# Two local-attention stacks: 48 rows in one sequence, each row's feed-forward cut into pieces beside the heads of later rows, weights loaded by parts

## The chip, the core and the metric

The kernel runs on one core of one Trainium2 chip. The metric is the device time of one execution in microseconds (us), the median of several executions. Below, PE is the matmul engine (TensorE), DVE is VectorE, ACT is ScalarE, POOL is GpSimd, and SP is the queue that issues the DMAs.

## What is computed

The input is 8 rows of 256 tokens with 128 features, in float32. Four blocks follow each other. Blocks 1 and 2 (0-based) end in a stack of six local-attention layers, and these two stacks are what the change is about. Cut to what matters:

```python
DIM, DEPTH, HEADS, DIM_HEAD, WINDOW = 128, 6, 16, 64, 32
DIM_INNER = 341

def attn_layer(x, Wqkv, qs, ksc, Wo):      # x is 8 rows of 256 x 128
    q, k, v = split(x @ Wqkv)              # 128 -> 3 * 1024, 16 heads of 64
    q, k = l2norm(q) * qs, l2norm(k) * ksc
    q, k = rotate(q), rotate(k)            # cos and sin tables, with a scale
    out = local_attention(q, k, v)         # window of 32, looks one window back
    return out @ Wo                        # 1024 -> 128

def ffn_layer(x, g, bln, W1, b1, W2, b2):
    xn = layernorm(x) * g + bln
    a, gate = split(xn @ W1 + b1)          # 128 -> 2 * 341
    return a * gelu(gate) @ W2 + b2

for i in range(DEPTH):
    x = attn_layer(shift_tokens(x), ...) + x
    x = ffn_layer(shift_tokens(x), ...) + x
```

The eight rows of a layer don't depend on each other. Row b of layer d+1 needs only row b of layer d.

## The kernel before

The stacks are `windowed_transformers`. Its inner `run(number)` emits one stack; it runs twice. The activations stand in the SBUF tile `Y`, one slice for each of the 8 rows. Work is ordered by hand: each engine has its own program, and the engines meet through semaphores. A **turn** is one row in one layer; turns count through a stack.

**The attention of a row** has two parts that overlap with its neighbours'.

- *Preparation* is spread over the eight pairs of heads of the row before it. PE makes 12 chunks of 512 columns of q, k and v (`pe_chunks`, L1518, two in each of the slots 0 to 5), ACT squares and copies them (L1661, L1665), DVE sums the squares and multiplies by the sine table (`dve_rotate`, L1762, L1770), POOL multiplies by the cosine table, adds, and scales the keys (`pool_prepare`, L1615, L1622, L1628), and PE transposes q and k (`pe_turn_qk`, L1544). In the slots 3 and 6 DVE takes 1/sqrt of the head norms by Newton steps (`dve_prepare`, L1786, then L704 to L710); each step waits for the step before. A short memset (L1788) then raises `rs_ready`, for which POOL's key scaling (L1628) waits.
- *The window* goes through eight pairs of heads p = 0 to 7: PE computes scores (L1450), DVE adds the mask and takes the maximum (L1731), ACT takes the exponential (L1638), PE transposes the probabilities (L1462, L1463), ACT copies them (L1647), PE spreads the reciprocals (L1477) and weighs the values (L1490). In pair 6 PE multiplies the previous row's context by Wo (`pe_out`, L1559). In pair 7 DVE adds that to `Y` (`dve_add`, L1794).

So `pe_window`, `act_window` and `dve_window` are the rows of one turn on the three engines. PE, ACT and DVE take their instructions strictly in the written order:

```python
for b in range(1, B - 1):
    pe_window(pe, turn + b, b % 2)
pe_window(pe, turn + B - 1, 1, last=True)
...
for b in range(B):
    pe_ff_step(pe, turn + b, b, b % 2, b == 0, b == B - 1, ...)
```

**The feed-forward** of a layer comes as a phase of its own, after the eighth row's attention: eight `pe_ff_step`s. A step shifts the next row's upper half of the features by one token (L1843, L1846), runs the 6 products with W1 (L1870), and the 6 with W2 (L1857). ACT shifts into `xn` (L1893), turns and scales the normed row (L276) and takes GELU (L1901). DVE takes mean and variance (L235 to L241), normalises (L245), multiplies the two halves (L1925), and adds to `Y` (L1918). POOL copies half a row (L1887) and takes the root of the variance (L252). The next layer's first row is prepared in this phase (`PREPARE_IN_FF`), and its other rows can't start in it. Exponential and GELU need different function tables in ACT: a table load stands ahead of each phase (L2020, L2028), so two in a layer.

**The loop.** Layers 0 to 4 of a stack run in a device loop (`Fori`), the sixth is written out behind it, without preparation in its feed-forward phase. SP loads the weights of a layer as whole tensors: Wqkv (1536 KB) once the layer before has finished its last preparation, and W1, W2 after its last feed-forward step.

The functions in full, with the profile's line numbers:

Of the kernel before, what the change touches and what calls it, by code (L numbers as in the profile page):

```python
# [81 lines left out]
def allocate(nc, ctx):  # L82
# [24 lines left out]
    c.next_row = sb("next_row", [P, HALVES, D])  # L107
# [1242 lines left out]
N_CHUNKS = len(CHUNK_ORDER)  # L1350
PE_CHUNK_SLOTS = {j: (2 * j, 2 * j + 1) for j in range(6)}
# [8 lines left out]
RSQRT_STEPS = 2 * (1 + NEWTON_STEPS)  # L1360


PREPARE_IN_FF = {2: ((0,), (1,)), 3: ((2,), ()), 4: ((3,), (4,)), 6: ((5, 6), ()), 7: ((7,), ())}

ATTN_FROM, FF_FROM = 2, B
SPAN = (P, P + WINDOW)
AT = (0, P)
FIRST_KEY = (0, P - WINDOW)


def windowed_transformers(nc, sem, c, name, io):
# [28 lines left out]
    hT = (c.hT, c.big[:, at:at + 3 * S].rearrange("p (k s) -> p k s", k=3))  # L1409
# [4 lines left out]
    ss = c.ss[:, :, :].rearrange("p t h -> p (t h)")  # L1414
    rs = tuple(c.rs[:, j, :, :].rearrange("p t h -> p (t h)") for j in range(2))

    def norms(buffer, g):
        return buffer[:, 32 * g:32 * g + 32]
# [4 lines left out]
    def whole_blocks(turned):  # L1423

        return turned.rearrange("p (t k) -> p t k", k=P + WINDOW)[:, :, 0:P]
# [4 lines left out]
    def chunk_bank(i):  # L1430
        return c.bank[7 - i % 2]

    def qkT_bank(i):

        return c.bank[7 - i % 2 if i < 2 or i >= 4 else 6 + i % 2]
# [3 lines left out]
    def pe_scores(pe, turn, j, p, first=False):  # L1439
        if p % 2 == 0:  # L1440

            pe.wait_ge(s.qT_copied, turn * 4 + p // 2 + 1)
            pe.wait_ge(s.kT_copied, turn * 4 + p // 2 + 1)
        if not first:

            pe.wait_ge(s.negmax_ready, turn * PAIRS + p)
        for t in range(HALVES):
            for side in range(2):
                q, k = [x[j][DH * side:DH * side + DH, p, :] for x in (qT, kT)]
                last = pe.matmul(c.bank[side][:, AT[t]:AT[t] + SPAN[t]], q[:, t * P:(t + 1) * P],  # L1450
                                 k[:, FIRST_KEY[t]:FIRST_KEY[t] + SPAN[t]], start=True, stop=True,
                                 skip_group_check=True)
        last.then_inc(s.scores_ready, 1)

    def pe_turn_probs(pe, turn, p, first):
        pe.wait_ge(s.probs_ready, turn * PAIRS + p + 1)
        if not (first and p == 0):

            pe.wait_ge(s.probsT_ready, turn * PAIRS + p)
        for side in range(2):  # L1460
            probs, out = c.pairs[:, 2 * (p % 4) + side, :], c.bank[2 + side]
            pe.transpose(out[:, 0:P], probs[:, 0:P], c.ident[:, :])  # L1462
            last = pe.transpose(out[:, P:2 * P], probs[:, P + WINDOW:2 * P + WINDOW], c.ident[:, :])  # L1463
        last.then_inc(s.probsT_in_psum, 1)

    def pe_shares(pe, turn, p, first):
        pe.wait_ge(s.recip_ready, turn * PAIRS + p + 1)
        if not (first and p < 2):

            pe.wait_ge(s.ctx_ready, turn * PAIRS + p - 1)  # L1470
        elif p == 1:

            pe.wait_ge(s.ff_added, FF_FROM + turn)
        rec = c.recip[:, 0, 4 * (p % 4):4 * (p % 4) + 4].rearrange("p (t h) -> p t h", t=HALVES)
        for t in range(HALVES):
            for side in range(2):
                pe.matmul(c.bank[4 + p % 2][DH * side:DH * side + DH, S + t * P:S + (t + 1) * P],  # L1477
                          rec[:, t, side:side + 1].broadcast_to((P, DH)), c.ident[:, :], start=True, stop=True,
                          skip_group_check=True)

    def pe_weigh(pe, turn, j, p):
        pe.wait_ge(s.probsT_ready, turn * PAIRS + p + 1)
        pe.wait_ge(s.prev_ready, turn * PAIRS + p + 1)
        if p == 0:
            pe.wait_ge(s.chunk_copied, (turn + 1) * N_CHUNKS)
        out = c.bank[4 + p % 2]
        for kt, q0, q1 in ((0, 0, P + WINDOW), (1, P, S)):
            at = 0 if kt == 0 else P + WINDOW
            for side in range(2):
                last = pe.matmul(out[DH * side:DH * side + DH, q0:q1], V[j][:, kt, 2 * p + side, :],  # L1490
                                 c.pairsT[:, 2 * (p % 2) + side, at:at + q1 - q0], start=(kt == 0), stop=(kt == 1),
                                 skip_group_check=True)
        last.then_inc(s.ctx_in_psum, 1)

    def pe_xT(pe, q, alone):
        pe.wait_ge(s.row_copied, q + 1)
        if alone:

            pe.wait_ge(s.attn_added, ATTN_FROM + q)
        for t in range(HALVES):  # L1500
            last = pe.transpose(c.bank[6][:, t * P:(t + 1) * P], c.next_row[:, t, :], c.ident[:, :])
        last.then_inc(s.rowT_in_psum, 1)

    def pe_chunks(pe, q, slot, alone):
        for i in PE_CHUNK_SLOTS.get(slot, ()):
            t, k = CHUNK_ORDER[i]
            if i == 0:
                pe.wait_ge(s.xT_ready, q + 1)
            if i < 2 and not alone:

                pe.wait_ge((s.qT_copied, s.kT_copied)[i], q * 4 - 1)
            elif i in (6, 7) and not alone:
                pe.wait_ge((s.qT_copied, s.kT_copied)[i - 6], q * 4)
            elif i >= 2 and CHUNK_ORDER[i - 2][1] < QK_CHUNKS:
                pe.wait_ge(s.chunk_rotated, q * ROTATED + QK_ORDER.index(CHUNK_ORDER[i - 2]) + 1)
            elif i >= 2:
                pe.wait_ge(s.chunk_copied, q * N_CHUNKS + i - 1)
# [30 lines left out]
    def pe_prepare(pe, q, slot, alone, first):  # L1548
        if slot == 0 and alone:
            pe_xT(pe, q, True)  # L1550
# [702 lines left out]
```

## Time and profile before

| | |
|---|---|
| median of 3 executions | 6789.9 us (6783.5 to 6796.6) |
| the profiled execution | 6798.7 us |
| its span, first to last instruction | 6797.0 us |
| PE busy | 5769.4 us, 85% of the span |
| DVE busy | 4295.0 us, 63% |
| ACT busy | 4171.8 us, 61% |
| POOL busy | 2486.0 us, 37% |
| granted clock of PE, mean | 0.936 of full speed |
| first stack, first `dve_add` to last feed-forward add | from 810.0 to 3136.5 us |
| second stack, the same | from 3435.6 to 5773.0 us |

Busy shares are averages over stages with different limits. The change is in the two stacks alone, so only their stretches are read. A stack is a repeated turn, so it is enough to know what one turn takes, how often it runs, and what stands between. The granted clock of PE has two levels, 1.0 (2.4 GHz) and 0.5 (1.2 GHz).

### The profile page before, as it was taken

The numbers are of one execution on the slowest core, as the hardware profiler recorded it, in microseconds if no ns is written. First come the engines' busy times: TensorE is split into PE (matmuls) and PEld (weight loads), VectorE is DVE, ScalarE is ACT, GpSimd is POOL, SyncE is SP. The second block draws the span as 40 slices with busy tenths as digits, with TensorE's granted clock in tenths as the row PEclk, the third lists the DMA queues.
The fourth block names the chain that finished last, engine by engine and source line by source line (L and its number), as shares of the span: only waits on it lengthen the run. The fifth ranks groups of instructions, "written<-read, shape, count | busy, mean of one in ns | idle before, by whom it ended". The sixth has DMA issues, their size and how long they took to land. (4 is left out here: it accounts for less than half of the span.)

```text
span 6797.0 us, 132994 instructions
## 1 busy us (share of the span) xinstructions
PE 5769.4 (85%) x41538; PEld 4249.7 (63%) x41538; DVE 4295.0 (63%) x17058; ACT 4171.8 (61%) x14046; POOL 2486.0 (37%) x2090
## 2 busy tenths in 40 slices
PE   8884798988989898896598898989889898787989
PEld 7773465666656566564366565666656566566778
DVE  4453775767767576774576775757767576444432
ACT  5511675857758586673386775858768586454643
POOL 0000553645445364550354554635455353000000
PEclk9995899999999999997699998999999999888999
DMA  0000000000000000000000000000000000000000
GB/s 10 20 1 2 19 2 18 2 14 5 12 8 2 18 2 15 5 1 3 19 2 14 5 2 18 2 18 2 15 5 2 18 1 2 4 1 3 1 26 7
DMA packets 22465, 54.76 MB, mean 8 GB/s; under 512 B 6728, under 2 KB 16208, under 8 KB 19536
## 3 DMA queue, kind: packets, MB, share of 16 engines
q1 hardware_dynamic: 21712, 45.65, 2.0%
q8 instruction: 358, 5.87, 0.4%
q14 instruction: 395, 3.24, 0.2%
HBM read 44.60 MB, written 1.05 MB: 7 GB/s over the span
## 5 line engine op out<-in xcount | busy, mean ns | idle before, releaser
L1518 PE MATMUL bank<-wA,next_rowT 128*128 128x512 f32 x2304 | 1255.4, 658 | 280.1 <-DVE turnB L1770 199.6
L1615 POOL TENSOR_TENSOR turnA<-raw,ropes 128x512 f32<-128x512 f32 x768 | 969.1, 1272 | 1000.8 <-ACT raw L1665 960.4
L1638 ACT ACTIVATE pairs<-pairs,negmax 128x128 f32<-128x128 f32 (+1 forms) x3072 | 1251.0, 433 | 65.2 <-DVE negmax L1731 63.1
L1731 DVE CUSTOM_DVE_ANT_0 pairs<-bank,bands,rs 128x128 f32<-128x128 f32 (+1 forms) x3072 | 943.5, 363 | 283.2 <-PE bank L1450 263.6
L1622 POOL TENSOR_TENSOR qk<-turnA,turnB 128x512 f32<-128x512 f32 x768 | 969.3, 1272 | 0.0
L1518 PEld LDWEIGHTS bank<-wA,next_rowT 128*128 128x128 f32 x2304 | 389.3, 196 | 774.8 <-DVE turnB L1770 465.6
L1647 ACT ACTIVATE pairsT<-bank 128x256 f32<-128x256 f32 x1536 | 522.5, 407 | 441.1 <-PE bank L1463 441.1
L252 POOL TENSOR_TENSOR rstd<-vareps,neg_half 128x2 f32<-128x2 f32 x152 | 106.2, 699 | 1791.8 <-DVE vareps L241 1791.8
L1638 ACT ACTIVATION_READ_ACCUMULATOR pairs<-pairs,negmax 128x1 f32 x3072 | 669.5, 218 | 0.0
L1628 POOL TENSOR_TENSOR qk<-qk,rs 128x1024 f32<-128x1024 f32 x192 | 365.1, 1902 | 728.5 <-DVE recip L1788 728.5
L1770 DVE TENSOR_TENSOR turnB<-bank,ropes 128x512 f32<-128x512 f32 x768 | 522.4, 680 | 0.0
L1477 PE MATMUL bank<-ident,recip 128*64 128x128 f32 x6144 | 508.3, 287 | 0.0
L563 ACT ACTIVATE pairs<-bank,negmax 128x256 f32<-128x256 f32 (+1 forms) x768 | 329.6, 435 | 279.1 <-DVE negmax L536 279.0
L536 DVE TENSOR_REDUCE negmax<-bank 128x1 f32<-128x256 f32 (+1 forms) x768 | 255.6, 374 | 351.6 <-PE bank L475 228.3
L1544 PE MATMUL bank<-ident,qk 128*128 128x128 f32 x3072 | 451.0, 286 | 28.1 <-ACT big L1668 12.6
L1665 ACT ACTIVATE raw<-bank 128x512 f32<-128x512 f32 x768 | 469.1, 611 | 0.0
L1544 PEld LDWEIGHTS bank<-ident,qk 128*128 128x128 f32 x3072 | 345.4, 145 | 159.9 <-issue 68.2
L1462 PE MATMUL bank<-ident,pairs 128*128 128x128 f32 x1536 | 388.6, 279 | 58.6 <-ACT pairs L1638 57.5
L472 PE MATMUL bank<-kT,qT 128*128 128x256 f32 (+1 forms) x1536 | 389.6, 370 | 24.8 <-DVE qT L525 24.8
L1477 PEld LDWEIGHTS bank<-ident,recip 128*64 128x64 f32 x6144 | 322.5, 136 | 130.6 <-issue 130.6
L1463 PE MATMUL bank<-ident,pairs 128*128 128x128 f32 x1536 | 382.8, 276 | 0.0
L1450 PE MATMUL bank<-kT,qT 64*128 64x128 f32 (+1 forms) x3072 | 307.4, 320 | 84.2 <-issue 48.3
(266 smaller groups left out, 11942.1 us busy)
## 6 DMA issues: line engine op xcount, KB each, us to landing
wA<-in_wt_wqkv SPq DMA_DIRECT2D x12, 1536.0 KB, 6.1
wB<-in_wt_wo SPq DMA_DIRECT2D x12, 512.0 KB, 3.2
wC<-in_wt_w SPq DMA_DIRECT2D x12, 341.0 KB, 3.4
wD<-in_wt_w SPq DMA_DIRECT2D x12, 192.0 KB, 3.4
big<-in_e_up SPq DMA_DIRECT2D x1, 2048.0 KB
big<-in_e_down SPq DMA_DIRECT2D x1, 2048.0 KB
scl<-in_wt_scales SPq DMA_DIRECT2D x12, 128.0 KB, 7.4
X<-in_x SPq DMA_DIRECT2D x8, 128.0 KB, 2.3
```

Of the source, the lines that this page charges most:

```text
L472: last = pe.matmul(out[:, at:at + n], c.qT[:, 1 + h % 4, t * P:(t + 1) * P], c.kT[:, 0, 0:n], start=True, stop=not self.causal, skip_group ...
L1462: pe.transpose(out[:, 0:P], probs[:, 0:P], c.ident[:, :])
L1477: pe.matmul(c.bank[4 + p % 2][DH * side:DH * side + DH, S + t * P:S + (t + 1) * P], rec[:, t, side:side + 1].broadcast_to((P, DH)), c.iden ...
L1518: pe.matmul(chunk_bank(i)[:, :], c.next_rowT[:, t * P:(t + 1) * P], wqkv[:, k * 512:(k + 1) * 512], start=True, stop=True).then_inc(s.chun ...
L1544: done = pe.transpose(qkT_bank(i)[:, (2 * k + t) * P:(2 * k + t + 1) * P], c.qk[:, t, which, at:at + P], c.ident[:, :])
L1615: g.tensor_tensor(c.turnA[:, m % 2, :].rearrange("p (h d) -> p h d", h=8), c.raw[:, m % 4, :].rearrange("p (h d) -> p h d", h=8), cos, ALU ...
L1622: g.tensor_tensor(c.qk[:, t, k // 2, (k % 2) * 512:(k % 2) * 512 + 512], c.turnA[:, m % 2, :], c.turnB[:, m % 4, :], ALU.add).then_inc(s.s ...
L1638: last = a.activation(tile, tile, ACT.Exp, scale=-1.0, bias=c.negmax[:, 2 * p + side, t:t + 1], accum_out=c.pair_sums[:, p % 4, t, side:si ...
L1647: last = a.activation(whole_blocks(whole), c.bank[2 + side][:, 0:2 * P].rearrange("p (t k) -> p t k", t=HALVES), ACT.Identity)
L1665: last = a.activation(c.raw[:, m % 4, :], src, ACT.Identity)
L1731: last = v.tensor_tensor_reduce(c.pairs[:, 2 * (p % 4) + side, AT[t]:AT[t] + SPAN[t]], c.bank[side][:, AT[t]:AT[t] + SPAN[t]], c.bands[:, ...
L1770: v.tensor_tensor(out, turned, sin.unsqueeze(1).broadcast_to((P, 8, 2, DH // 2)), ALU.mult).then_inc(s.chunk_rotated, 1)
```

## The change

The `Fori` loop and the feed-forward phase go. A stack is now one sequence of 48 turns T, all written out. Beside the heads of turn T run the preparation of turn T+1, as before, and the feed-forward of the row of two turns earlier, f = T-2, in pieces:

- pair 2: PE shifts (`pe_shift`), ACT copies (`act_shifted`)
- pair 3: DVE takes the statistics (`dve_ff_stats`), puts the two variances behind the head norms, runs the same Newton steps over 34 columns instead of 32, raises `rs_ready` by the memset as before, and then normalises with four instructions of 64 columns (`dve_ff_normalise`). POOL's part in the feed-forward is gone.
- pair 4: PE transposes the normed row (`pe_turn_normed`), ACT scales it
- pair 6: PE runs 4 of the 6 products with W1 (`pe_gates`), ACT loads the GELU table and takes GELU
- pair 7: PE runs the other 2 (`pe_linear`), DVE makes the three products with the gates
- pair 1 of the next turn: PE multiplies by W2 (`pe_ff_out`), DVE adds to `Y`

PE reads the row to be turned straight from `Y`, so POOL's copy to `next_row` goes. Probabilities are copied by one ACT instruction of 512 columns for a pair instead of two of 256. The feed-forward uses PSUM bank 3, the transposed probabilities share bank 2. Behind turn 47 two rows' feed-forward are left for a tail. SP loads Wqkv in six parts, each when the last chunk of the old layer that reads it is done. The diff, cut to this:

```diff
-PREPARE_IN_FF = {2: ((0,), (1,)), 3: ((2,), ()), 4: ((3,), (4,)), 6: ((5, 6), ()), 7: ((7,), ())}
+WEIGHT_ORDER = (2, 0, 4, 3, 1, 5)
+TURNS = DEPTH * B
...
         def pe_window(pe, T):
...
+                if p == 6 and has_turn(T - 2):
+                    pe_gates(pe, T - 2, (s.qT_copied, (T + 1) * 4 + (1 if following else 0)))
                 if p >= 1:
                     pe_shares(pe, T, p - 1)
                     pe_weigh(pe, T, p - 1)
...
+                if p == 1 and has_turn(T - 3):
+                    pe_ff_out(pe, T - 3)
+                if p == 2 and has_turn(T - 2):
+                    pe_shift(pe, T - 2)
+                if p == 4 and has_turn(T - 2):
+                    pe_turn_normed(pe, T - 2)
+                if p == 6 and has_turn(T - 1):
+                    pe_out(pe, T - 1, (s.kT_copied, (T + 1) * 4 + (1 if following else 0)))
+                if p == 7 and has_turn(T - 2):
+                    pe_linear(pe, T - 2)
                 if following:
                     pe_prepare(pe, T + 1, p, False)
...
+        def act_copy_probs(a, T, p):
+            a.wait_ge(s.probsT_in_psum, T * PAIRS + p + 1)
+            a.activation(whole_blocks(c.pairsT[:, 2 * (p % 2):2 * (p % 2) + 2, :]),
+                         c.bank[2][:, :].rearrange("p (n k) -> p n k", n=4), ACT.Identity).then_inc(s.probsT_ready, 1)
...
+        def act_gelu(a, f):
+            a.wait_ge(s.gates_in_psum, f + 1)
+            if has_turn(f - 1):
+                a.wait_ge(s.hidden_ready, f * 3)
+            for k, (at, n) in enumerate(FF_CHUNKS):
+                src = c.bank[7][0:n, 0:S] if k == 2 else ff_bank[0:n, k * S:(k + 1) * S]
+                a.activation(gelu[0:n, k, :], src, ACT.Gelu, bias=c.cols[0:n, 5 + k:6 + k]).then_inc(s.gelu_ready, 1)
...
+        def dve_ff_stats(v, f):
+            v.wait_ge(s.attn_added, f + 1)
+            v.wait_ge(s.shifted_ready, f + 1)
+            for t, n, src in ff_halves(f):
+                last = v.bn_stats(ff_stats[:, t, n, :], src)
+            step.after(last, v)
+            for t in range(HALVES):
+                last = v.bn_aggr(ff_mv[:, t, :], ff_stats[:, t, :, :].rearrange("p n k -> p (n k)"))
+            step.after(last, v)
+            step.after(v.tensor_scalar(ss[:, ff_var], ff_mv[:, :, 1], LN_EPS, None, ALU.add), v)
+        def dve_ff_normalise(v, f, rstd):
+            for t, n, src in ff_halves(f):
+                last = v.tensor_scalar(c.xn[:, t, n * (D // 2):(n + 1) * (D // 2)], src, ff_mv[:, t, 0:1],
+                                       rstd[:, t:t + 1], ALU.subtract, ALU.mult)
+            last.then_inc(s.normed, 1)
...
         def dve_prepare(v, q, slot, f=None):
             if slot in DVE_RSQRT_SLOTS:
...
+                    dve_ff_stats(v, f)
+                    dve_roots(v, ss[:, 0:32 + HALVES], rs[q % 2][:, 0:32 + HALVES])
                 v.memset(c.recip[:, 0, 31:32], 0.0).then_inc(s.rs_ready, 1)
+                if f is not None:
+                    dve_ff_normalise(v, f, rs[q % 2][:, ff_var])
...
+                for d in range(layer_of(T0), layer_of(T1)):
...
+                    for k in WEIGHT_ORDER:
+                        if not first:
+                            sp.wait_ge(s.chunk_in_psum, (T - 1) * N_CHUNKS + CHUNK_ORDER.index((1, k)) + 1)
+                        sp.dma_start(wqkv[:, k * 512:(k + 1) * 512],
+                                     w["wqkv"][d][:, k * 512:(k + 1) * 512]).then_inc(wqkv_loaded[k], 16)
...
+                pe_scores(pe, T0, 0)
+                pe_scores(pe, T0, 1)
+                for T in range(T0, T1):
+                    pe_window(pe, T)
+                pe_tail(pe)
```

Three places of the written order follow. In brackets is what an instruction waits for.

DVE, end of pair 3 and start of pair 4 of a turn in the middle. Before (the rows between are the other Newton steps):

```order
L1756 COPY kT<-bank 128x512
L1786 TENSOR_SCALAR ss<-ss 128x32
...
L710 SCALAR_TENSOR_TENSOR rs<-newton 128x32
L57 REGISTER_ALU
L1788 MEMSET recip 128x1
L1740 RECIPROCAL recip<-pair_sums 128x4
L1745 TENSOR_TENSOR ctxT<-bank,shares 128x256
```

Now:

```order
L1864 COPY big<-bank 128x512 [waits wt_kT_in_psum]
L1915 BN_STATS big<-Y 128x6 [waits wt_shifted_ready,wt_attn_added,wt_chunk_rotated]
...
L1918 BN_AGGR big<-big 128x2 [waits wt_steps]
...
L1894 TENSOR_SCALAR big<-big 128x34 [waits wt_steps]
...
L1959 MEMSET recip 128x1 [waits wt_steps]
L1924 TENSOR_SCALAR xn<-Y,big 128x64 x2
L1924 TENSOR_SCALAR xn<-xn,big 128x64 x2
L1848 RECIPROCAL recip<-pair_sums 128x4 [waits wt_probs_ready]
```

The statistics now stand ahead of the Newton steps, and the four normalising instructions stand between the memset that frees POOL and pair 4's work.

PE, from the Wo products of pair 6 to the transposed probabilities of the next turn's pair 0. Before:

```order
L1559 MATMUL bank<-wB,ctxT 128x128 x15
L1462 MATMUL bank<-ident,pairs 128x128 [waits wt_probsT_ready,wt_probs_ready]
...
L1450 MATMUL bank<-kT,qT 128x128 [waits wt_negmax_ready]
...
L1490 MATMUL bank<-pairsT,big 64x128 x2
L1544 MATMUL bank<-ident,qk 128x128 [waits wt_kT_copied,wt_sum_ready]
```

Now:

```order
L1574 MATMUL bank<-wB,ctxT 128x128 x15
L1480 MATMUL bank<-ident,pairs 128x128 [waits wt_probsT_ready,wt_probs_ready]
...
L1468 MATMUL bank<-big 128x128 [waits wt_negmax_ready]
...
L1603 MATMUL bank<-xT,wC 128x256 [waits wt_gelu_ready]
...
L1562 MATMUL bank<-ident,qk 128x128 [waits wt_hidden_ready,wt_sum_ready]
```

Two W1 products stand between the weighing of pair 6 and the q and k transposes.

ACT, the same stretch. Now (before, neither table load nor GELU stood here):

```order
L1737 ACTIVATE shares<-bank 128x256 [waits wt_ctx_in_psum]
L1786 ACT_TABLE_LOAD [waits wt_hidden_ready]
L1786 ACTIVATE big<-bank,cols 128x256 [waits wt_gates_in_psum]
L1786 ACTIVATE big<-bank,cols 128x256
L1786 ACTIVATE big<-bank,cols 85x256
L1732 ACTIVATE pairsT<-bank 128x4x128 [waits wt_probsT_in_psum]
L1725 ACT_TABLE_LOAD
L1725 ACTIVATE pairs,pair_sums<-pairs,negmax 128x128 [waits wt_negmax_ready]
```

A table load stands ahead of GELU and another between the copy of pair 7's probabilities and the next exponentials, once in each turn.

## Rows read from the trace of the kernel before

**Rows 1.** Timeline, DVE: start us, us, engine, line, op, idle before and releaser.

```profile
809.96 0.42 DVE L1794 TENSOR_TENSOR Y<-Y,bank 128x256 f32<-128x256 f32 x1 [0.57 <-PE bank L1559]
...
3015.32 0.42 DVE L1794 TENSOR_TENSOR Y<-Y,bank 128x256 f32<-128x256 f32 x1 [0.66 <-PE bank L1559]
...
3056.43 0.42 DVE L1794 TENSOR_TENSOR Y<-Y,bank 128x256 f32<-128x256 f32 x1 [0.66 <-PE bank L1559]
...
3086.32 0.42 DVE L1794 TENSOR_TENSOR Y<-Y,bank 128x256 f32<-128x256 f32 x1 [4.60 <-PE bank L1559]
...
3136.53 0.42 DVE L1918 TENSOR_TENSOR Y<-Y,bank 128x256 f32<-128x256 f32 x1 [1.76 <-PE bank L1857]
...
3435.59 0.42 DVE L1794 TENSOR_TENSOR Y<-Y,bank 128x256 f32<-128x256 f32 x1 [0.47 <-PE bank L1559]
...
5773.00 0.42 DVE L1918 TENSOR_TENSOR Y<-Y,bank 128x256 f32<-128x256 f32 x1 [1.76 <-PE bank L1857]
```

**Rows 2.** Windows: stretch, its us, busy us of PE, PEld, DVE, ACT, POOL, PEclk, DMA.

```profile
891.70:932.70 41.00, 38.29 (x316) 26.47 (x315) 32.61 (x135) 32.99 (x115) 24.32 (x20) 1.00 0.01 2
```

**Rows 3.** Timeline, PE, a feed-forward step of the sixth layer.

```profile
3109.84 2.86 PE L1870 MATMUL bank<-xT,wC 128*128 128x256 f32 x12
3112.53 1.50 PE L1857 MATMUL bank<-wD,hT 128*128 128x128 f32 x12
3113.87 0.38 PE L263 MATMUL bank<-ident,xn 128*128 128x128 f32 x2
```

**Rows 4.** Timeline, PE, pair 4 of the turn of rows 2.

```profile
918.45 2.32 PE L1518 MATMUL bank<-wA,next_rowT 128*128 128x512 f32 x4 [1.00 <-DVE turnB L1770]
```

**Rows 5.** Timeline, DVE, then POOL, pairs 3 and 4 of that turn.

```profile
916.35 0.06 DVE L1788 MEMSET recip<- 128x1 f32 x1
...
917.71 0.68 DVE L1770 TENSOR_TENSOR turnB<-bank,ropes 128x512 f32<-128x512 f32 x1
...
916.49 1.90 POOL L1628 TENSOR_TENSOR qk<-qk,rs 128x1024 f32<-128x1024 f32 x1 [3.88 <-DVE recip L1788]
918.35 2.50 POOL L1615 TENSOR_TENSOR turnA<-raw,ropes 128x512 f32<-128x512 f32 x2
```

**Rows 6.** Timeline, DVE, statistics of a feed-forward row.

```profile
3115.45 0.49 DVE L235 BATCH_NORM_STATS2 stats<-xn 128x6 f32<-128x128 f32 x2 [0.96 <-POOL xn L1887]
...
3116.26 0.17 DVE L241 TENSOR_SCALAR vareps<-mv 128x2 f32<-128x2 f32 x1
```

**Rows 7.** Line L245 (min/median/max ns); then timeline, DVE and POOL, first preparation.

```profile
L245 DVE TENSOR_SCALAR xn<-xn,mv,rstd x192: 332/344/1287, 1050.4 to 5764.1; 128x128 f32<-128x128 f32 x192
...
708.72 1.20 DVE L708 TENSOR_TENSOR newton<-newton 128x32 f32<-128x32 f32 x1
...
708.60 2.49 POOL L1622 TENSOR_TENSOR qk<-turnA,turnB 128x512 f32<-128x512 f32 x2
```

**Rows 8.** Windows, two neighbouring stretches, second turn of the second layer.

```profile
1176.00:1179.40 3.40, 1.50 (x16) 1.12 (x14) 2.97 (x14) 1.05 (x3) 2.40 (x2) 1.00 0.00 0
1179.40:1182.80 3.40, 3.40 (x24) 2.77 (x23) 1.24 (x8) 1.72 (x7) 0.00 (x0) 0.51 0.03 5
```

**Rows 9.** Timeline, PE, then ACT: from pair 7 to the next turn's pair 0.

```profile
891.73 0.27 PE L1462 MATMUL bank<-ident,pairs 128*128 128x128 f32 x1
...
894.96 0.27 PE L1462 MATMUL bank<-ident,pairs 128*128 128x128 f32 x1
...
892.36 0.66 ACT L1647 ACTIVATE pairsT<-bank 128x256 f32<-128x256 f32 x2 [3.81 <-PE bank L1463]
892.91 0.40 ACT L1638 ACTIVATE pairs<-pairs,negmax 128x128 f32<-128x128 f32 x1
...
894.50 0.37 ACT L1653 ACTIVATE shares<-bank 128x256 f32<-128x256 f32 x1
```

**Rows 10.** Timeline, ACT, the table load ahead of the feed-forward phase.

```profile
1052.78 1.28 ACT L2028 ACT_TABLE_LOAD   x1
1054.08 0.20 ACT L2028 ACTIVATE cols<-neg_half 128x1 f32<-128x1 f32 x1
```

More of the change, by code:

```diff
@@ L1423, in whole_blocks, with side_bank @@
     def whole_blocks(turned):
-        return turned.rearrange("p (t k) -> p t k", k=P + WINDOW)[:, :, 0:P]
+        return turned.rearrange("p a (t k) -> p (a t) k", k=P + WINDOW)[:, :, 0:P]
     def part_of(buffer, pp):
         return buffer[:, 2 * pp:2 * pp + 2, :].rearrange("p k s -> p (k s)")
-    def chunk_bank(i):
+    def side_bank(i):
         return c.bank[7 - i % 2]
[L1433 to L1447, printed above, removed]
-            for side in range(2):
[L1449 to L1464, printed above, removed]
@@ L1481, in pe_weigh @@
[L1481 to L1517, printed above, removed]
-            pe.matmul(chunk_bank(i)[:, :], c.next_rowT[:, t * P:(t + 1) * P], wqkv[:, k * 512:(k + 1) * 512], start=True,
-                      stop=True).then_inc(s.chunk_in_psum, 1)
@@ L1896, in act_ff_step @@
-    def act_ff_step(a, turn, b, last, beside):
-        if not last:
-            act_shifted(a, turn + 1)
-        for k, (at, n) in enumerate(FF_CHUNKS):
-            a.wait_ge(s.ff_in_psum, turn * 3 + k + 1)
-            a.activation(c.ctxT[0:n, k, :],
-                         c.bank[k][0:n, S:2 * S], ACT.Gelu,
-                         bias=c.cols[0:n, 5 + k:6 + k]).then_inc(s.gelu_ready, 1)
-        beside(b, 0)
-        if not last:
-            ff_norm.scalar(a, turn + 1)
-        beside(b, 1)
@@ L2006, in _ @@
-                prepare(layer0, range(PAIRS))
-                with g.Fori(layer0, layer1 - 1) as d:
-                    layer(d, False)
-                layer(layer1 - 1, True)
+                for q in range(T0, T1):
+                    for slot in range(PAIRS):
+                        pool_prepare(g, q, slot)
             @block.scalar
             def _(a):
-                def prepare(turn, slots):
-                    for slot in slots:
-                        act_prepare_early(a, turn, 0, slot)
-                        act_prepare(a, turn, 0, slot)
@@ L2033, in _ @@
-                prepare(layer0 * B, range(PAIRS))
-                with a.Fori(layer0, layer1 - 1) as d:
-                    layer(d, False)
-                layer(layer1 - 1, True)
+                a.activation(c.cols[:, 30:31], c.neg_half[:, 0:1], ACT.Exp)
+                act_xT(a, T0)
+                for i in range(N_CHUNKS):
+                    act_copy_chunk(a, T0, i)
+                act_copy_q(a, T0, 0)
+                act_copy_q(a, T0, 1)
+                act_probs(a, T0, 0, 0)
+                act_probs(a, T0, 0, 1)
@@ L2082, in _ @@
-                step = dve_steps(v, layer0 * B)
-                prepare(layer0, step, range(PAIRS))
-                step.end()
-                with v.Fori(layer0, layer1 - 1) as d:
-                    layer(d, False)
-                layer(layer1 - 1, True)
+                dve_tables(v, T0)
+                for slot in range(PAIRS):
+                    for m in DVE_ROTATE_SLOTS.get(slot, ()):
+                        dve_rotate(v, T0, m)
+                    dve_prepare(v, T0, slot)
+                    if slot == 6:
+                        dve_copy_k(v, T0, 0)
@@ L2089, in windowed_transformers @@
+                dve_negmax(v, T0, 0)
+                dve_negmax(v, T0, 1)
+                for T in range(T0, T1):
+                    dve_window(v, T)
+                dve_tail(v)
     return run
```

970 lines of the change are left out of this document (508 added, 462 removed).

## The prediction

> **What bounds the kernel now.** I read the views in the order of the rows. First, DVE's timeline at the adds to `Y`: they cut the execution into turns. Stack 1 takes 3136.53 − 809.96 = 2326.6 us from its first attention add to its last feed-forward add, stack 2 takes 5773.00 − 3435.59 = 2337.4, and the adds at 3015.32 and 3056.43 show a turn that is already written out: 41.11 us [rows 1]. Then the window of one looped turn: 41.00 us, with PE busy for 38.29 at full clock (1.00), DVE 32.61, ACT 32.99, POOL 24.32 [rows 2]. PE is the bound, and 2.7 us of a turn are its waits. So work that is put into a turn isn't free because "an engine has room": what goes to PE is added whole, and what goes to DVE is free until PE waits for it.
>
> The place where PE waits for DVE is pair 4: chunk 8 comes 1.00 us late, released by the sine product `turnB` [rows 4]. DVE's end of pair 3 shows the cause, a chain of Newton steps, the memset at 916.35, then the next pair's work to the sine product at 917.71; POOL's key scaling starts 0.14 after the memset, takes 1.90, and two cosine products follow it without a gap, 2.50 [rows 5]. There is no slack behind the Newton steps.
>
> Measured against the span, 6797.0 of 6798.7 us: the sum below is a difference, and I put it on the median, 6789.9, which lies 8.8 below the profiled execution. A measurement of this kernel tells 0.2% (13.6 us) from no change.
>
> **The change, part by part, for one turn T'.**
>
> 1. *What is gone*: the feed-forward phase. A stack becomes 45 full turns (2 to 46), one last turn, and a tail.
> 2. *PE's share of a feed-forward row.* W1's 12 products take 3112.53 − 3109.84 = 2.69, W2's take 3113.87 − 3112.53 = 1.34 [rows 3]. The six narrow shift products, at no more than W2's 0.11 each, take 0.6. All stand between products of a saturated PE, so 4.63 are added. The two transposes (about 0.2) fall where PE waits anyway.
> 3. *Small waits*, an estimate of 0.3: the row's transpose waits for the hidden products to be read, and a new layer's scales are copied in the stream.
>    So far 41.11 + 4.63 + 0.3 = 46.04.
> 4. *Statistics on DVE*, ahead of the Newton steps: a row of 256 tokens took 3116.26 + 0.17 − 3115.45 = 0.98 [rows 6], in four parts of 64 columns now instead of two. Between 1.0 and 1.5; I take 1.2. They lengthen the chain that ends in chunk 8's wait, so all of it is path.
> 5. *Normalising*, four instructions between the memset and pair 4's work. Alone, one of 128 columns takes 0.344, so four of 64 about 0.9. But line L245 has a maximum of 1287 ns [rows 7]: in this trace it was about that long each time POOL was at work, 10 of 10, and a 32-column Newton product took 1.20 while POOL ran 708.60 to 711.09 [rows 7], against some 0.19 elsewhere. An instruction of DVE with SBUF operands alone waited for POOL's current one to end, so DVE got one through for each of POOL's. Here the memset has just released POOL: 1.90, then 1.25, then 1.25 of work [rows 5]. The first of the four may get in ahead, the second ends with the key scaling, the others with a cosine product each. They end between 3.5 and 4.7 behind the memset; I take 4.1. Both the row's transpose and, over the sine product, chunks 8 and 9 wait for them. Bounds: 0.9 (never held) and 4.7.
>    The Trainium skill, "SBUF — State Buffer", section "SBUF: two separate sides", says the same: DVE and GpSimd share a port pair under an exclusive lock, which lasts for the whole instruction. By that rule, the trace agrees (1.20 against 0.19); were the lock fair only at the end of POOL's whole queue, it would be the 4.7.
> 6. *The clock.* In 1176.0 to 1179.4 PE was busy 1.50 of 3.40 us, and the granted clock of the next 3.40 us was 0.51, that is 1.2 GHz, with PE busy throughout [rows 8]. There a work of 1.7 took 3.4. A turn with over 5 us of new idle time in front of chunk 8 will show this each time: 0 to 1.7, and I take 1.4, since most of what follows the stall is PE work.
> 7. *ACT's table loads*, 1.28 each with the next instruction 0.02 behind [rows 10], twice a turn. The critical one stands between pair 7's copy and pair 0's exponentials. ACT's chain from PE's transposes of pair 7: 0.63 to the copy, 0.55 for it, 1.30 for the load, 1.59 for the exponentials (892.91 to 894.50), 4.07 in all; PE needs 894.96 − 891.73 = 3.23 [rows 9], and the two W1 products that now stand there add 0.90 (a third of 2.69): 4.13. A tie, hidden by those products; without them it would cost 0.8. ACT's total, 33.0 + 2.6 + about 2.5 for GELU and copies, stays below T'.
>    The Trainium skill, "ScalarE: Activation LUTs", section "What ACT_TABLE_LOAD costs", adds a drain of about 1380 ns to a load of 1283, 2.66 us for a switch. The trace has the 1283 but not the drain ahead of the next instruction (0.02). By the page T' would be 1.4 longer; this is a rival below.
> 8. *At nothing*: POOL's work that goes (POOL has 16 us of idle a turn), the copy of the probabilities in one instruction, and Wqkv in parts, whose bytes are the same and which have several turns to land in. An instruction stream that isn't looped: turns 41.11 against 41.00, in the sum already.
>
> T' = 46.04 + 1.2 + 4.1 + 1.4 = 52.7.
>
> *A stack now*: 45 × 52.7 = 2371.5, less 1.3 for the first of them, which has no W2 yet. The last turn has no preparation: 3086.32 − 3056.43 = 29.9 before [rows 1], with feed-forward pieces 35. Behind it stood 3136.53 − 3086.32 = 50.2 with the last Wo and eight feed-forward steps; six fewer, at 4.6 of PE each, would leave 22, but two rows can't cover each other's chains: 38, between 22 and 50. Together 2443.2. Against 2326.6 and 2337.4 that is +116.6 and +105.8, **+222 us, so 7012, and I say 7010**. Each us of T' is 90 us, and break-even lies at T' = 50.2.
>
> **Rivals.**
>
> - *Not held (ends faster).* DVE's four independent instructions follow each other without a wait, unlike the Newton steps of rows 7, and may all slip in before POOL's, which starts 0.14 late. Then normalising costs 0.9 and half the clock loss: T' = 46.04 + 2.1 + 0.7 = 48.8, 3.9 below, −351 us: **6661**. What decides is whether pair 4 starts less than 1.6 us later than I have it (T' under 50.2). For it: no row shows independent instructions in this place. Against: L245's, two to a row and independent, were held 10 of 10.
> - *Held once.* POOL's key scaling holds one, and the others get in together between it and the cosine products: ends 2.5 behind the memset, T' = 46.04 + 3.7 + 1.4 = 51.1, −144: **6868**.
> - *The table switch costs more than its row.* If something behind it drains, 1.4 is added to a chain that already ties: T' = 54.1, +126: **7138**. The page named in 7 would have it so; rows 10 speak against it.
> - *The waits fill up.* The 2.7 us that PE waits in a turn take the added work in, and DVE and POOL don't collide: T' = 46, **6410**. Against it: the wait at pair 4 lies on DVE's chain, which grows.
>
> **How the numbers follow.** My forecast 0.42, not held 0.28, held once 0.17, table switch 0.04, waits filled 0.03, something else 0.06. The range reaches from not held (6661, less some for a tail or a sum of small waits that is shorter) to my forecast with the full wait of 4.7 and its clock (T' = 53.7, 7100): 6640 to 7110. It leaves out the table switch, filled waits, and most of the rest. Since both signs hold much of the chance: the forecast's own range, with 3.5 to 4.7 for normalising and a clock loss of 1.0 to 1.7, is 6920 to 7110. Faster by over 0.2%: 0.28 + 0.03 + 0.03 = 0.34. Within 0.2%: 0.04, a T' between 50.05 and 50.35. Slower: 0.62.
>
> **What will show it.** The spacing of the adds to `Y` is T' itself: 52.7, against 48.8 or 51.1. The duration of the normalising instructions: one at about 0.2 and three above 1 in my case, and POOL's key scaling and cosine products beside them. PE's idle time ahead of chunk 8 or of the row's transpose: 5 to 6 us by me, 3 if not held. The granted clock: a stretch of 0.5 behind that wait in every turn. PE's busy time in a turn at full clock: 43. ACT's gap behind a table load: 0.02, not 1.4. Transposes of pair 0 released by PE's own order, not by ACT. I am wrong if the normalising rows are short, or if PE doesn't wait there, or if the wait at another place (pair 0, behind the table load) is the longest.

## The result, and the profile after

| | before | changed |
|---|---|---|
| median | 6786.7 us (6779.2 to 6796.6, 4 executions) | 7085.5 us (7083.5 to 7086.4, 4 executions) |
| ratio | | 1.0439 (95% interval 1.0421 to 1.0457) |
| span of the profiled execution | 6797.0 us | 7083.7 us |
| mean granted clock of PE | 0.936 | 0.905 |

The changed kernel is 4.4% slower. Its time lies inside the range (6640 to 7110) and on the forecast side, 75 us above the point of 7010. That range was wide enough for the faster rivals too, so the turn's spacing below tests the forecast better than the time does.

The first view is again DVE's timeline at the adds to `Y` (L1905 attention, L1947 feed-forward): start, duration, and in brackets the idle time before with its releaser.

```profile
804.80 0.42 DVE L1905 TENSOR_TENSOR Y<-Y,bank 128x256 f32<-128x256 f32 x1 [0.44 <-PE bank L1574]
...
1497.55 0.42 DVE L1905 TENSOR_TENSOR Y<-Y,bank 128x256 f32<-128x256 f32 x1 [2.58 <-PE bank L1574]
...
1551.16 0.42 DVE L1905 TENSOR_TENSOR Y<-Y,bank 128x256 f32<-128x256 f32 x1 [2.58 <-PE bank L1574]
...
3209.48 0.42 DVE L1905 TENSOR_TENSOR Y<-Y,bank 128x256 f32<-128x256 f32 x1 [2.58 <-PE bank L1574]
...
3286.57 0.42 DVE L1947 TENSOR_TENSOR Y<-Y,bank 128x256 f32<-128x256 f32 x1 [3.02 <-PE bank L1631]
3579.43 0.42 DVE L1905 TENSOR_TENSOR Y<-Y,bank 128x256 f32<-128x256 f32 x1 [0.66 <-PE bank L1574]
...
6059.88 0.42 DVE L1947 TENSOR_TENSOR Y<-Y,bank 128x256 f32<-128x256 f32 x1 [2.94 <-PE bank L1631]
```

These rows answer to [rows 1]. Stack 1 now takes 2481.8 us against 2326.6, stack 2 takes 2480.5 against 2337.4: +298 together. A turn lasts 52.75, 53.6 or 54.06 in a pattern of three, 53.50 in the mean of 44 turns.

Where does PE wait in a turn? PE's timeline at pair 4, the answer to [rows 4]:

```profile
1525.56 0.66 PE L1505 MATMUL bank<-pairsT,big 128*64 128x160 f32 x8
1530.85 0.55 PE L1598 MATMUL bank<-ident,xn 128*128 128x128 f32 x2 [4.63 <-DVE xn L1924]
1532.83 2.08 PE L1539 MATMUL bank<-wA,next_rowT 128*128 128x512 f32 x2 [1.43 <-DVE turnB L1878]
```

The old wait of 1.00 has become 4.63 for the normalised row and 1.43 for the sine product, 6.06 in all. What DVE and POOL did in that time, to be read against [rows 5]:

```profile
1526.23 0.31 DVE L1924 TENSOR_SCALAR xn<-Y,big 128x64 f32<-128x64 f32 x1
1526.26 0.06 DVE L1959 MEMSET recip<- 128x1 f32 x1
1526.46 1.90 DVE L1924 TENSOR_SCALAR xn<-Y,big 128x64 f32<-128x64 f32 x1
1528.27 2.52 DVE L1924 TENSOR_SCALAR xn<-xn,big 128x64 f32<-128x64 f32 x2
1530.72 0.16 DVE L1848 RECIPROCAL recip<-pair_sums 128x4 f32<-128x4 f32 x1
...
1526.39 1.91 POOL L1715 TENSOR_TENSOR qk<-qk,big 128x1024 f32<-128x1024 f32 x1 [5.99 <-DVE recip L1959]
1528.27 2.48 POOL L1702 TENSOR_TENSOR turnA<-raw,ropes 128x512 f32<-128x512 f32 x2
```

The first normalising instruction takes 0.31. The second takes 1.90, as long as POOL's key scaling (1.91); the third and fourth share 2.52 with POOL's two cosine products (2.48). One of DVE's goes through for each of POOL's. The last ends at 1530.79, 4.53 behind the memset at 1526.26. Per line, over both stacks (count, min/median/max ns):

```profile
L1924 DVE TENSOR_SCALAR xn<-Y,big x192: 307/312/1897, 831.1 to 6048.2; 128x64 f32<-128x64 f32 x192
L1924 DVE TENSOR_SCALAR xn<-xn,big x192: 305/1300/1301, 833.2 to 6048.6; 128x64 f32<-128x64 f32 x192
```

In the second line 180 of the 192 took about 1300. The other 12 belong to the last three rows of each stack, beside which no next row is prepared. Last, windows: the first is about that turn, the others are parts of it (us, then busy us of PE, PEld, DVE, ACT, POOL, then granted clock, DMA):

```profile
1501.29:1555.05 53.76, 46.05 (x350) 31.98 (x348) 40.58 (x151) 37.78 (x116) 23.72 (x18) 0.94 0.00 1
1525.00:1531.00 6.00, 1.37 (x20) 1.06 (x18) 5.79 (x13) 2.58 (x11) 4.35 (x3) 1.00 0.00 0
1531.00:1537.80 6.80, 5.37 (x14) 2.47 (x15) 6.49 (x20) 2.80 (x6) 2.97 (x3) 0.50 0.00 0
1537.80:1544.60 6.80, 6.18 (x49) 4.03 (x48) 3.32 (x14) 5.38 (x19) 4.52 (x4) 1.00 0.00 1
```

PE worked for 1.37 of 6.00 us, and the next 6.8 us were granted 0.50 of the clock, 1.2 GHz. From the first attention add to the last feed-forward add of the first stack the half clock lasted 387 us, against 140 in the kernel before.

ACT's table loads, in the stretch before the next turn's first exponentials:

```profile
1551.60 0.60 ACT L1732 ACTIVATE pairsT<-bank 128x512 f32<-128x512 f32 x1 [1.30 <-PE bank L1481]
1552.21 1.28 ACT L1725 ACT_TABLE_LOAD   x1
1553.51 0.40 ACT L1725 ACTIVATE pairs<-pairs,negmax 128x128 f32<-128x128 f32 x1
```

The exponential starts 0.02 behind the load, as in [rows 10]; ACT had waited 1.30 for PE before the copy, so ACT is not late here. Ahead of the load there is no gap either: the copy ends at 1552.20.

### The profile page after: what moved, and what is told of

The parts are those of the page before. It is cut to its first block and busy times, and to the rows that moved or that the text cites. A ratio compares the mean times of both kernels' runs of the same rounds, so it can differ in the third digit from the quotient of the medians.

```text
span 7083.7 us, 123716 instructions
## 1 busy us (share of the span) xinstructions
PE 5881.7 (83%) x41538; PEld 4283.7 (60%) x41538; DVE 4656.3 (66%) x17416; ACT 4350.7 (61%) x13414; POOL 2328.6 (33%) x1802
## 5 line engine op out<-in xcount | busy, mean ns | idle before, releaser
L1539 PE MATMUL bank<-wA,next_rowT 128*128 128x512 f32 x2304 | 1294.3, 689 | 216.8 <-DVE turnB L1878 138.4
L1839 DVE CUSTOM_DVE_ANT_0 pairs<-bank,bands,big 128x128 f32<-128x128 f32 (+1 forms) x3072 | 942.0, 362 | 244.9 <-PE bank L1468 241.1
L1539 PEld LDWEIGHTS bank<-wA,next_rowT 128*128 128x128 f32 x2304 | 432.8, 210 | 661.8 <-issue 321.6
L1715 POOL TENSOR_TENSOR qk<-qk,big 128x1024 f32<-128x1024 f32 x192 | 366.3, 1908 | 1121.6 <-DVE recip L1959 1121.6
L251 POOL TENSOR_TENSOR rstd<-vareps,neg_half 128x2 f32<-128x2 f32 x56 | 39.1, 698 | 1803.0 <-DVE vareps L240 1803.0
L1725 ACT ACTIVATION_READ_ACCUMULATOR pairs<-pairs,negmax 128x1 f32 x3072 | 626.0, 204 | 0.0
L1732 ACT ACTIVATE pairsT<-bank 128x512 f32<-128x512 f32 x768 | 467.7, 609 | 201.7 <-PE bank L1481 201.7
L1745 ACT ACTIVATE big<-bank 128x512 f32<-128x512 f32 x384 | 230.3, 600 | 417.5 <-PE bank L1539 417.1
L1598 PE MATMUL bank<-ident,xn 128*128 128x128 f32 x192 | 61.2, 416 | 437.6 <-DVE xn L1924 437.6
L1737 ACT ACTIVATE shares<-bank 128x256 f32<-128x256 f32 x768 | 292.8, 381 | 190.4 <-PE bank L1505 186.4
```

The costliest lines, as they stand in the source:

```text
L1539: pe.matmul(side_bank(i)[:, :], c.next_rowT[:, t * P:(t + 1) * P], wqkv[:, k * 512:(k + 1) * 512], start=True, stop=True).then_inc(s.chunk ...
L1715: g.tensor_tensor(keys, keys, norms_of(rs[q % 2], m)[:, :, 1, :].unsqueeze(3) .broadcast_to((P, HALVES, 8, DH)), ALU.mult).then_inc(s.keys ...
L1725: last = a.activation(tile, tile, ACT.Exp, scale=-1.0, bias=c.negmax[:, 2 * p + side, t:t + 1], accum_out=c.pair_sums[:, p % 4, t, side:si ...
L1732: a.activation(whole_blocks(c.pairsT[:, 2 * (p % 2):2 * (p % 2) + 2, :]), c.bank[2][:, :].rearrange("p (n k) -> p n k", n=4), ACT.Identity ...
L1839: last = v.tensor_tensor_reduce(c.pairs[:, 2 * (p % 4) + side, AT[t]:AT[t] + SPAN[t]], c.bank[side][:, AT[t]:AT[t] + SPAN[t]], c.bands[:, ...
```

## The experiments

The theory: the feed-forward's PE work is a small, fixed price; what makes the change slow is the place of the normalising instructions behind POOL's release, where they are held, and the clock that PE loses over the wait. The rivals: any work on DVE's chain costs this wherever it stands; the table loads; PE's added work is itself absorbed.

### Normalise before POOL is released

```diff
-                v.memset(c.recip[:, 0, 31:32], 0.0).then_inc(s.rs_ready, 1)
                 if f is not None:
                     dve_ff_normalise(v, f, rs[q % 2][:, ff_var])
+                v.memset(c.recip[:, 0, 31:32], 0.0).then_inc(s.rs_ready, 1)
```

> The changed kernel with the four normalising instructions ahead of the memset that releases POOL instead of behind it; the same instructions. Theory (they are held by POOL's port use): they take 0.25 to 0.3 us each again, so PE's wait ahead of the normed row and chunk 8 shrinks by about 3.5 us, and most of the clock loss goes with it: the spacing of the adds falls from 53.5 to about 48.5 (47.8 to 50), the time to about 6640 (6590 to 6770). Rival 1 (it is the added work on DVE's chain as such, wherever it stands): spacing and time as in the changed kernel, 7085 within 30. Rival 2 (POOL, released 1 us later, becomes the bound): the waits move to POOL's sums, time above 6900.

Measured: 6697.6 us, ratio to the kernel before 0.9855 (0.9838 to 0.9871). The same instructions in another order, and 388 us less; the change is now faster than the kernel before. Its timeline on DVE, POOL and PE:

```profile
1424.98 0.54 DVE L1924 TENSOR_SCALAR xn<-Y,big 128x64 f32<-128x64 f32 x2
1425.43 0.53 DVE L1924 TENSOR_SCALAR xn<-xn,big 128x64 f32<-128x64 f32 x2
...
1426.07 1.90 POOL L1715 TENSOR_TENSOR qk<-qk,big 128x1024 f32<-128x1024 f32 x1 [6.89 <-DVE recip L1961]
...
1426.02 0.44 PE L1598 MATMUL bank<-ident,xn 128*128 128x128 f32 x2 [1.11 <-DVE xn L1924]
1428.01 1.22 PE L1539 MATMUL bank<-wA,next_rowT 128*128 128x512 f32 x1 [1.55 <-DVE turnB L1878]
```

All four take 0.98 together, and PE's first wait is 1.11 instead of 4.63. The spacing is 49.13 in the mean, 4.37 less; 3.5 of that is the hold, the rest is clock (half clock 150 us in the first stack instead of 387). Rival 1 falls: it isn't the work. Rival 2 falls too: PE's two waits here end with DVE, not with POOL. 6698 against the expected 6640 is inside its range, but part of the clock loss stays. Of 44 turns 10 had no half clock, and such a turn takes 48.15:

```profile
1445.62:1493.77 48.15, 43.72 (x348) 30.69 (x347) 36.82 (x151) 37.47 (x114) 23.71 (x18) 1.00 0.01 2
```

The mean is 0.98 above that; waits of 1.11 + 1.55 are still there.

### Only the four instructions, in the kernel before

```diff
             v.memset(c.recip[:, 0, 31:32], 0.0).then_inc(s.rs_ready, 1)
+            if g == 0:
+                for n in range(4):
+                    v.tensor_scalar(c.extra[:, n, :], c.extra[:, 4, :], c.extra[:, 4, 0:1], c.extra[:, 4, 1:2],
+                                    ALU.subtract, ALU.mult)
```

In the second kernel the added lines stand ahead of the memset. Both have a scratch tile besides, zeroed once a stack.

> The kernel before, plus four tensor_scalar of 64 columns on a scratch tile, right behind the memset of pair 3 that releases POOL; nothing waits for them but DVE's own order. Theory (held once for each of POOL's instructions): one short, three of 1.3 to 1.9 us; PE's wait at chunk 8 grows by 4.4 less nothing, with clock loss about 4.5 to 6 us a turn on 84 turns outside the feed-forward phases: 7170 to 7290. Rival (only their own work, 0.9 to 1.0 a turn): about 6870.

> The same four instructions in the kernel before, ahead of that memset. Theory: not held, 0.9 to 1.0 a turn on 84 turns, no more clock loss than before or little: 6865 (6850 to 6900). Rival (any DVE work there costs what it costs in the changed kernel): as with the four behind, above 7150.

Measured, in 2 executions each: 7390.1 us behind the memset (ratio 1.0876, 1.0854 to 1.0898), 6927.9 ahead of it (1.0195, 1.0175 to 1.0216). The kernel before had 6797.2 beside them. So instructions that nothing reads cost 593 us in one place and 131 in the other, one memset apart. DVE and POOL with the four behind:

```profile
895.29 0.31 DVE L1792 TENSOR_SCALAR extra<-extra 128x64 f32<-128x64 f32 x1
895.31 0.06 DVE L1789 MEMSET recip<- 128x1 f32 x1
895.51 4.34 DVE L1792 TENSOR_SCALAR extra<-extra 128x64 f32<-128x64 f32 x3
...
895.45 1.91 POOL L1629 TENSOR_TENSOR qk<-qk,rs 128x1024 f32<-128x1024 f32 x1 [3.91 <-DVE recip L1789]
897.32 2.48 POOL L1616 TENSOR_TENSOR turnA<-raw,ropes 128x512 f32<-128x512 f32 x2
```

Ahead of the memset none of the 384 took more than 318 ns. The mechanism is shown, but both times lie above their ranges (7170 to 7290 and 6850 to 6900), and for the same two reasons. I had counted nothing for the feed-forward phase, in which the next layer's first row is prepared: from the last attention add of a layer to its last feed-forward add it took 79.4 us in most layers before, 86.1 with the four behind and 80.9 with the four ahead. And the clock: with the four behind, a turn went from 41.0 to 47.1 to 47.7, over 6 for an added chain of 4.5. With the four ahead, 33 of 60 turns cost about the 0.9 that I had put down (41.9 to 42.1), and 27 cost 2.2 to 2.5.

### No function tables

```diff
-                a.activation(gelu[0:n, k, :], src, ACT.Gelu, bias=...)
+                a.activation(gelu[0:n, k, :], src, ACT.Identity, bias=...)
```

> The changed kernel with Identity in place of GELU, so that no function table is loaded in a turn; the rest, with its durations, is the same. The activation of the feed-forward is left out by this. Theory (the loads are hidden by the W1 products but for a tie): spacing down by 0.2 at most, time 7070 (7050 to 7085). Rival (the switch costs more than its row shows, or the chain from pair 7 to pair 0 is ACT's): spacing down by 0.8 to 1.5, 6950 to 7015.

Measured: 7082.3 us, 3 below the changed kernel. ACT's busy time in a turn falls from 37.8 to 34.9, and the spacing from 53.50 to 53.46. The loads are hidden, within that little.

### PE kept busy through the wait

```diff
+            pe.wait_ge(s.shifted_ready, f + 1)
+            for n in range(36):
+                pe.transpose(ff_bank[:, 0:P], c.ident[:, :], c.ident[:, :])
             pe.wait_ge(s.normed, f + 1)
-            pe.wait_ge(s.shifted_ready, f + 1)
```

> The changed kernel, in which PE makes 36 transposes of the identity (about 3.9 us at full clock), whose results nobody reads, in the wait of 4.6 us ahead of the normed row's transposes. No other wait changes. Theory (the half clock behind that wait comes from the wait, and costs 1.5 to 2.3 us a turn): the clock stays at 1.0 there, the spacing falls from 53.5 to about 51.5, the time by 90 x 2 to 6905 (6870 to 6960). Rival (the half clock has another cause, or what it slows is hidden): spacing and time as in the changed kernel, 7085, or more.

Measured: 6989.6 us, 96 below the changed kernel. PE's rows at pair 4, then the windows of two turns of it:

```profile
1565.07 4.15 PE L1597 MATMUL bank<-ident 128*128 128x128 f32 x36
1569.86 0.44 PE L1600 MATMUL bank<-ident,xn 128*128 128x128 f32 x2 [0.63 <-DVE xn L1926]
1571.84 1.12 PE L1539 MATMUL bank<-wA,next_rowT 128*128 128x512 f32 x2 [1.54 <-DVE turnB L1880]
...
1484.78:1536.53 51.75, 47.81 (x384) 34.60 (x383) 40.40 (x151) 37.48 (x114) 23.78 (x18) 1.00 0.01 1
1536.53:1589.72 53.19, 49.38 (x384) 35.50 (x383) 39.73 (x151) 37.65 (x114) 23.74 (x18) 0.97 0.00 1
```

Useless work in the wait makes the kernel faster, so the wait does cost clock. Of 44 turns, 20 take 51.75, at full clock; that is the spacing of the change with the hold, and without the clock loss, 1.75 below its 53.50. As a check, the turn at full clock with the normalising first, 48.15, is 3.60 below it, and the normalising there is 3.55 shorter. But the other 24 turns still take 52.7 to 53.2, the longest at 0.97, as in the second window. The mean is 52.44, and the time lies above its range: 96 us were gained where 180 were expected. The half clock in the first stack fell from 387 us to 85. Why the waits of 0.63 and 1.54 that are left do it in some turns, and not in the others, stays open.

### Less of W2

This kernel leaves out two of the three parts of the W2 product; it stands on the one with the normalising first (6697.6).

```diff
-                for k, (at, n) in enumerate(FF_CHUNKS):
-                    m = n + (k == 2)
-                    last = pe.matmul(...)
+                at, n = FF_CHUNKS[2]
+                m = n + 1
+                last = pe.matmul(...)
```

> The kernel with the normalising ahead of the release (6698 us), with 8 of the 12 W2 products of a row left out: only the third part of the hidden row is multiplied. Theory (PE's feed-forward work is added whole to a turn, 0.11 a product): spacing down by 0.9, time down by 80 to 6618 (6600 to 6640). Rival (PE's waits take that work in): 6698 within 14. Between them if a wait further on grows.

Measured: 6633.8 us, 64 less (57 by the ratios to the kernel before). The time is inside the theory's range, but the spacing fell by 0.49, not 0.9, so the theory holds in part. PE's waits in a turn didn't grow (4.20 against 4.27), so they don't take the work in. What grew is the half clock, from 150 to 205 us in the first stack, and no turn is left without it. The likely reading is that the rest of the gain was given back to the clock; I haven't run this on a kernel whose clock is full throughout, which would show it.

### Shortening DVE's chain, twice

First, the statistics ahead of the late copy of the keys, in the 0.7 us where DVE waits for PE:

```diff
+                if p == 3 and following and has_turn(T - 2):
+                    dve_ff_stats(v, T - 2)
                 if p in COPY_LATE_QKT_SLOTS:
                     dve_copy_k(v, T, COPY_LATE_QKT_SLOTS[p])
```

> The kernel with the normalising ahead of the release, and the statistics moved ahead of the late copy of the keys in pair 3, where DVE waits about 0.7 us for PE. Theory (DVE's chain from there to the sine product of pair 4 is the bound): chunk 8 comes 0.7 us earlier, spacing down by 0.7 to 1.1, time 6620 (6590 to 6640). Rival (the keys' copy comes 0.4 later, and PE waits for pair 6's scores instead): 6700 to 6735.

Measured: 6568.3 us (ratio 0.9677, 0.9661 to 0.9693).

Second, the sine product ahead of the sum of squares (`dve_rotate`), on the same base; the sum is waited for once per group of four, before the Newton steps:

```diff
-            v.tensor_reduce(norms_of(ss, k % 2)[:, t, k // 2, :], sq[m % 4]..., AX, ALU.add)
...
                             ALU.mult).then_inc(s.chunk_rotated, 1)
+            last = v.tensor_reduce(norms_of(ss, k % 2)[:, t, k // 2, :], sq[m % 4]..., AX, ALU.add)
+            if m % 4 == 3:
+                step.after(last, v)
```

> The kernel with the normalising ahead of the release, with the sine product ahead of the sum of squares in each of the eight steps of a preparation. Theory (each chunk that waits for a sine product gets it 0.6 us earlier): chunk 8 comes 0.6 earlier, spacing down by 0.6 to 1.0, time 6630 (6600 to 6650). Rival (ACT's copy, which the sine product waits for, comes later than the square, so nothing is gained): 6698 within 14.

Measured: 6568.4 us (0.9676, 0.9660 to 0.9692). PE's rows at pair 4, of the first and then of the second:

```profile
1496.44 0.44 PE L1598 MATMUL bank<-ident,xn 128*128 128x128 f32 x2 [0.27 <-DVE xn L1924]
1498.43 3.58 PE L1539 MATMUL bank<-wA,next_rowT 128*128 128x512 f32 x4 [1.55 <-DVE turnB L1878]
```

```profile
1499.99 0.44 PE L1598 MATMUL bank<-ident,xn 128*128 128x128 f32 x2 [1.10 <-DVE xn L1926]
1501.39 2.32 PE L1539 MATMUL bank<-wA,next_rowT 128*128 128x512 f32 x4 [0.95 <-DVE turnB L1877]
```

The first move takes 0.84 from one wait, the second 0.60 from the other. Each brought 129 us (about 120 by the ratios to the kernel before) where 78 and 68 were expected, and both times lie below their ranges: the spacing fell by 1.36 and 1.33, more than the waits did. The turns at full clock fell by less, from 48.15 to 47.37 and to 47.60. The rest is clock again: 77 and 60 us of half clock in the first stack, against 150.

Then both:

> The kernel with the normalising ahead of the release, with the statistics in the copy's wait and the sine product first. Theory (one chain on DVE, on which 0.7 and 0.6 us add up): spacing at full clock 48.2 - 0.7 - 0.6 = 46.9, no half clock left to win but that of a few turns, time 6495 (6475 to 6530). Rival (the second of the two moves finds another bound, for each alone had most of its gain from the clock): 6550 to 6568.

Measured: 6485.7 us (0.9547, 0.9531 to 0.9563). The two gains add up: the spacing is 46.83 turn after turn, 1.32 below 48.15, and the window of one is at full clock:

```profile
1456.39:1503.22 46.83, 43.78 (x348) 30.61 (x347) 36.04 (x151) 37.50 (x114) 23.71 (x18) 1.00 0.01 2
```

### ACT normalises

On top of both moves, DVE makes the two biases (−mean × rstd) ahead of the memset, and ACT the normalised row; the row is turned in pair 5 (the last three rows of a stack stay with DVE):

```diff
-                    dve_ff_normalise(v, f, rs[q % 2][:, ff_var])
+                    step.after(v.scalar_tensor_tensor(out=ff_bias, in0=ff_mv[:, :, 0], scalar=-1.0,
+                                                      in1=rs[q % 2][:, ff_var], op0=ALU.mult, op1=ALU.mult), v)
...
+                    last = a.activation(c.xn[...], src[...], ACT.Identity,
+                                        scale=rs[q % 2][:, 32 + t:33 + t], bias=ff_bias[:, t:t + 1])
```

> The same, with ACT normalising (four instructions with scale and bias per row, after pair 5's exponentials) instead of DVE, which makes the two biases alone; the normed row is turned in pair 5. Theory (DVE's chain is still the bound, and gets 0.7 to 0.8 us shorter): spacing 46.2, time 6430 (6410 to 6470). Rival (the wait at chunk 8 is used up, or ACT's added 1.0 us delays the copies that chunks and sine products wait for): 6485 or more.

Measured: 6438.2 us, ratio 0.9477 (0.9461 to 0.9493), the fastest of all. PE's chunk 8 and the transposes of the normed row, and the window of a turn:

```profile
1480.26 2.31 PE L1540 MATMUL bank<-wA,next_rowT 128*128 128x512 f32 x4 [0.97 <-DVE turnB L1890]
...
1484.96 0.44 PE L1599 MATMUL bank<-ident,xn 128*128 128x128 f32 x2
...
1450.63:1496.93 46.30, 43.60 (x348) 30.61 (x347) 35.29 (x147) 38.52 (x118) 23.71 (x18) 1.00 0.01 1
```

The transposes no longer wait. Chunk 8 waits 0.97, as it did in the kernel before (1.00, [rows 4]), in a turn that holds a whole feed-forward row besides. PE is busy for 43.6 of 46.3 us, and its waits are 2.7, the same as before the change.

## Why the prediction was right, and where it was off

- *What bounds the kernel* held: PE, with its largest wait at pair 4 on DVE's chain: 4.63 + 1.43 = 6.06, just above the 5 to 6 forecast. At full clock, 0.84 and 0.60 taken from those waits gave 0.78 and 0.55 in the spacing.
- *PE's work, small waits and statistics* (46.04 + 1.2 = 47.24) were sized right as a sum. The full-clock turn of the filled kernel, 51.75, less the 4.53 of the hold, leaves 47.22; the statistics took 1.15 (1522.36 to 1523.51). In part that is luck: PE's busy time in a turn at full clock is 43.8, where 43 was forecast, and what is left of the 47.2 for waits is 3.4, where 2.7 + 0.3 + 1.2 = 4.2 stood in the sum. The two misses cancel.
- *Normalising held* was the right mechanism, chosen over "not held" and "held once". [rows 7] showed it on other instructions, and the independent ones in this place behaved alike: held, one for each of POOL's. Its size was 4.53, not 4.1: I let three instructions end somewhat before POOL's third, but the last ends with it. The bound of 4.7 held. By the Trainium skill, "SBUF — State Buffer", section "SBUF: two separate sides", the lock lasts for the whole instruction; the trace agrees (1.90 beside 1.91). The same section names as its takers on DVE only instructions in a 2-port perf mode or with two SBUF inputs. That is narrower than the prediction's "SBUF operands alone", and the trace agrees: a sum of squares, with one SBUF input, isn't held (last section).
- *The clock* was the term most in need of a row. I took 1.4 from one stretch of 3.4 us at half clock; here a turn has 6.8 or 10.2 us of it. By the filled kernel's full-clock turns it costs 1.75. I had named 1.7 as the upper end, so it was just passed.
- Together T' came to 53.50 where 52.7 was forecast, 0.80 × 90 = 72 us. This is nearly the whole miss.
- *The last turn and the tail* took 3286.57 − 3209.48 = 77.1 instead of 73, +4 a stack. *Weights by parts*, costed at nothing, may have gained a little, which no run separates: the first chunk of stack 1 starts 7.8 us earlier (689.3 against 697.1), the first add 5.2, and from one stack to the other it is 292.9 instead of 299.1. With 76 us over on the two stacks and 11 under around them, the profiled pair differs by 286.7 where 222 were forecast.
- *The table loads* are hidden, as the sum of 4.13 against 4.07 had it; taking them out gave 3 us. The Trainium skill, "ScalarE: Activation LUTs", section "What ACT_TABLE_LOAD costs", gives a drain beside the load. No row here shows one, neither ahead of the next instruction (0.02) nor between the instruction before and the load (0.01), and the time without loads leaves no room for 1.38 us a turn on the path.
- *The waits fill up*, the rival against added PE work, is out for the change itself. The break-even at T' = 50.2 held: 49.13 a turn, with the normalising first, is faster than before, by 1.4%.

## What to carry to other kernels

Before elementwise work of DVE on SBUF operands is put anywhere, look at what POOL will be doing at that moment: the same four instructions cost 1 us ahead of POOL's release and 4.5 behind it, and the order of the two made the difference between 4.4% slower and 1.4% faster. Where PE is the bound and waits at one place in a repeated turn, price the wait with its clock: taking 0.6 to 0.8 us out of that wait gave 1.3 us a turn, about half of it clock. And follow the wait, not the busy shares: four small moves on one chain brought the changed kernel from 7085 to 6438 us, while PE's own work stayed.

## What was not expected of the hardware

- Once POOL is released with a queue of three instructions, DVE's independent ones, already queued, don't slip in together: the second, third and fourth each took as long as one of POOL's (1.90, then 2.52 for two beside 2.48), although DVE's first had started ahead of POOL and took 0.31.
- Not every DVE instruction on SBUF operands alone is held, as the prediction had put it. With the normalising first, the sum of squares reads and writes SBUF, runs beside POOL's key scaling (1426.07 to 1427.97), and takes its usual time, as does the sine product behind it, which reads PSUM. The kernel before showed it already, in the stretch of [rows 5], beside the key scaling from 916.49 to 918.39 (first line; the other two are of the kernel with the normalising first):

```profile
917.11 0.69 DVE L1762 TENSOR_REDUCE ss<-sq 128x8 f32<-128x512 f32 x1
...
1426.67 0.69 DVE L1870 TENSOR_REDUCE big<-sq 128x8 f32<-128x512 f32 x1
1427.27 0.68 DVE L1878 TENSOR_TENSOR turnB<-bank,ropes 128x512 f32<-128x512 f32 x1
```

- The loss of clock isn't proportional to the wait. With 4.63 + 1.43 us of waits at pair 4, half clock took 387 us of the first stack; with 1.11 + 1.55, 150; with 0.27 + 1.55, 77; with 1.10 + 0.95, 60; with 0.28 + 0.96, 24, all of it outside the full turns.
- 36 transposes whose results nobody reads, put into a wait, made a kernel faster by 96 us.
